# Identity products ahead of the first transpositions, keys before queries, and the second segment's rows normalised on GpSimd

## The reference

```python
xn = layernorm(x)                         # over 256, no scale or shift
q, k, v = split(xn @ Wqkv.T)              # 16 heads of 16; q scaled by 16 ** -0.5
# in each segment of 512 tokens every 8th token is a key: 64 keys for 512 queries
scores = q4 @ k4.T                        # within the segment
c = max(scores over each block of 64 queries, for each key)
w = exp(scores - c);  den = sum(w over keys) + 1e-10
att = (w @ v4 / den) @ Wout.T
ffn = relu(xn @ W1 + b1) @ W2 + b2        # 256 -> 1024 -> 256
out = x + att + ffn
```

## Time and profile before

| | us |
|---|---|
| median of three executions | 1058.35 |
| lowest, highest | 1057.06, 1059.67 |
| profiled execution, time | 1057.22 |
| profiled execution, span from first to last instruction | 1055.3 |
| busy in the span: TensorE, VectorE, ScalarE, GpSimd | 1040.6, 835.4, 648.7, 622.7 |

### The profile page before, as it was taken

How to read it: one execution, slowest core, us unless ns; L and a number is a source line. 1 busy time by engine, 2 the same in 40 slices (tenths; PEclk the granted TensorE clock), 3 DMA queues, 4 the chain that set the end, 5 groups by cost and what they waited for, 6 DMA issues and landing times.

```text
span 1055.3 us, 19263 instructions
## 1 busy us (share of the span) xinstructions
PE 1040.6 (99%) x5397; PEld 809.7 (77%) x5397; DVE 835.4 (79%) x1464; ACT 648.7 (61%) x1081; POOL 622.7 (59%) x491
## 2 busy tenths in 40 slices
PE   6999999999999999999999999999999999999998
PEld 4677778777787777787777787777877777877777
DVE  8977788778888887878878887788888878887753
ACT  5666666656666566665666656566665666656663
POOL 5456655665655666565656656556656565556564
PEclk9999999999999999999999999999999999999999
DMA  5168787787877787877778777879777788768744
GB/s 194 38 160 228 207 234 212 191 216 202 246 216 195 193 216 224 236 206 208 202 213 225 225 204 184 231 201 251 210 192 205 208 229 234 199 175 218 194 145 148
DMA packets 156359, 214.15 MB, mean 203 GB/s; under 512 B 27568, under 2 KB 96304, under 8 KB 156336
## 3 DMA queue, kind: packets, MB, share of 16 engines
q1 hardware_dynamic: 156192, 213.73, 74.4%
q10 hardware_dynamic: 144, 0.13, 0.0%
HBM read 100.01 MB, written 58.20 MB: 150 GB/s over the span
## 4 chain that ended last, share of the span: by engine, by line
PE 92%; DVE 3%; SPq 1%; DMA 1%; issue 1%; ACT 0%; DVEq 0%
PE h_bank L1109 40%; PE y_bank L1109 39%; PE s_banks L1184 5%; PE misc L1288 3%; PE s_banks L1288 3%; PE misc L1109 2%; DVE xn L882 1%; DVE s_max L899 1%; DMA q_pack<-q_hi 1%; DVE w_exp L905 0%; PE misc L1254 0%; PE misc L1226 0%; DMA k_dram<-k_lo 0%; SPq L417 0%; PE s_banks L1195 0%
## 5 line engine op out<-in xcount | busy, mean ns | idle before, releaser
L541 POOL TENSOR_TENSOR h_lo<-h_full,h_hi 128x512 fp32r<-128x512 f32 x256 | 336.9, 1317 | 371.0 <-ACT h_full L646 368.0
L652 ACT ACTIVATE w_exp<-w_exp 128x512 f32<-128x512 f32 x256 | 161.7, 633 | 244.1 <-DVE w_exp L905 242.2
L644 ACT ACTIVATE h_hi<-h_bank,b_cols 128x512 fp32r<-128x512 f32 x256 | 174.8, 683 | 67.7 <-PE h_bank L1109 62.2
L1109 PE MATMUL h_bank<-xt_hi,w_hi 128*128 128x512 f32 x512 | 206.4, 403 | 0.0
L1109 PE MATMUL h_bank<-xt_lo,w_hi 128*128 128x512 f32 x512 | 200.0, 391 | 0.0
L1109 PE MATMUL h_bank<-xt_hi,w_lo 128*128 128x512 f32 x512 | 199.6, 390 | 0.0
L1109 PE MATMUL y_bank<-h_hi,w_hi 128*128 128x512 f32 x496 | 193.4, 390 | 0.2 <-ACT w_exp L652 0.2
L1109 PE MATMUL y_bank<-h_hi,w_lo 128*128 128x512 f32 x496 | 193.1, 389 | 0.0
L1109 PE MATMUL y_bank<-h_lo,w_hi 128*128 128x512 f32 x496 | 193.1, 389 | 0.0
L899 DVE TENSOR_REDUCE s_max<-s_banks 128x8 f32<-128x512 f32 x252 | 169.5, 672 | 28.8 <-PE s_banks L1184 28.4
L905 DVE TENSOR_TENSOR w_exp<-s_banks,s_max 128x512 f32<-128x512 f32 x252 | 174.3, 692 | 10.9
(11 more groups left out here) (149 smaller groups left out, 1540.3 us busy)
## 6 DMA issues: line engine op xcount, KB each, us to landing
q_pack<-q_hi SPq DMA_DIRECT2D x240, 128.0 KB, 2.6
rden_rows<-rden_dram SPq DMA_DIRECT2D x128, 128.0 KB, 4.5
x_b<-x SPq DMA_DIRECT2D x32, 512.0 KB, 4.5
x_raw<-x SPq DMA_DIRECT2D x31, 512.0 KB, 4.8
yt_dram<-y_mem SPq DMA_DIRECT2D x124, 128.0 KB, 3.5
y_mem<-yt_dram SPq DMA_DIRECT2D x62, 256.0 KB, 4.0
out<-x_b SPq DMA_DIRECT2D x31, 512.0 KB, 3.1
q_pack<-q_lo SPq DMA_DIRECT2D x120, 128.0 KB, 2.5
```

Of the source, the lines that this page charges most:

```text
L541: pool.tensor_tensor(h_part[1][:, i % HBUF], h_full[:, i % HBUF], f32(h_part[0][:, i % HBUF]), ALU.subtract).then_inc(h_lo, 1)
L644: act.activation(h_part[0][:, i % HBUF], h_bank[i % 2][:], ACT.Relu, bias=b1_cols[:, i:i + 1]).then_inc(h_hi, 1)
L652: act.activation(w_exp[:, pair], w_exp[:, pair], ACT.Exp).then_inc(w_ready, 1)
L1109: mm = pe.matmul(ps, stationary[a], moving[b], start=start and c == 0 and n == 0, stop=stop and c == len(pairs) - 1 and n == 2, skip_group ...
```

## The change

In the order of the engines:

- TensorE: `raise_clock(count)` issues products of the f32 identity with itself into `h_bank[0]`, which nothing reads: ten before the keys' rows are transposed and two after. `transpose_k` is moved ahead of both halves of the queries. In `lead_step`, `second_product(0, 1)` and the last group of scores are moved ahead of the transposition of segment 1's rows.
- ScalarE: it drains the first key and value sums (`kv_drained`), between the hi parts of the transposed x and of w1. The keys' hi part and the queries' are moved ahead between the weight halves. In `lead_step` it writes segment 0's values into `v` (`first_values`, two copies), behind the second segment's `pair_keys_hi`.
- VectorE: `drain_kv`, `normalise(1, 1)` and `pair_values(-2, 0)` go. `mask_k` comes ahead of the statistics of segment 1, `keys_projected_lo` ahead of the queries' lo parts, and both of these are now in `first_step`. In `lead_step`, the lo part of w2's second half comes behind those of the transposed rows and the keys. A wait for `xn_ready` at 2 is added ahead of `mean_variance(2, 0)`.
- GpSimd: it no longer waits for `xn` before the lo part of w1's second half. In `lead_step` it normalises the rows of segment 1 (`second_rows_normalised`, four `tensor_scalar`) after two `hidden_lo`, and does all five `hidden_lo` before the memset of `q_pack`'s unused rows.

SyncE's code is unchanged.

```diff
--- before.py
+++ after.py
@@ -608,20 +608,31 @@
                     pool.wait_ge(w1_hi[half], 1)
                     if half == 1:
                         inverse_deviation(1, 1)
-                        pool.wait_ge(xn_ready, 2)
                     pool.tensor_tensor(w1_half(w1s[1], half), w1_half(w1_raw, half), f32(w1_half(w1s[0], half)),
                                        ALU.subtract).then_inc(w1_lo[half], 1)
                 pool.wait_ge(w2_hi[0], 1)
                 pool.tensor_tensor(w2_half(w2s[1], 0), w2_half(w2_raw, 0), f32(w2_half(w2s[0], 0)),
                                    ALU.subtract).then_inc(w2_lo[0], 1)
 
+            def second_rows_normalised():
+
+                pool.wait_ge(rstd_ready, 2)
+                pool.wait_ge(xt_psum, DH)
+                for t in range(T):
+                    op = pool.tensor_scalar(xn[:, t], x_raw[:, 1, t], mean_var[:, t, 0:1], rstd[:, t:t + 1],
+                                            ALU.subtract, ALU.mult)
+                op.then_inc(xn_ready, 1)
+
             def lead_step():
-                for i in range(4):
-                    hidden_lo(0, i)
-                pool.wait_ge(h_lo, 4)
+                hidden_lo(0, 0)
+                hidden_lo(0, 1)
+                second_rows_normalised()
+                hidden_lo(0, 2)
+                hidden_lo(0, 3)
+                hidden_lo(0, 4)
+                pool.wait_ge(h_lo, 5)
                 pool.memset(f32(q_pack[PR:P]).rearrange("p n t -> p (n t)"), 0.0).then_inc(pack_zeroed, 1)
                 pool.wait_ge(pack_zeroed, 2)
-                hidden_lo(0, 4)
                 inverse_deviation(2, 0)
                 hidden_lo(0, EARLY)
                 hidden_lo(0, EARLY + 1)
@@ -686,6 +697,18 @@
                 act.wait_ge(q_psum, (s + 2) * DH + m + 1)
                 act.copy(q_part[0][:, m], query_banks(s)[m][:]).then_inc(q_hi, 1)
 
+            def kv_drained(s):
+                act.wait_ge(kv_psum, s + 4)
+                act.copy(kv[:], key_banks(s)[1][:]).then_inc(kv_ready, 2)
+
+            def first_values():
+
+                act.wait_ge(kv_ready, 2)
+                act.wait_ge(masks_zero, 2)
+                for a in range(2):
+                    act.copy(v[a * KEYS:(a + 1) * KEYS, 0].rearrange("p n (d a) -> p n d a", a=2)[:, :, :, a],
+                             kv[0:KEYS, D:].rearrange("p (n a d) -> p n a d", a=2, d=HD)[:, :, a, :]).then_inc(v_ready, 1)
+
             def pair_keys_hi(s, par):
                 act.wait_ge(k_ready, s + 3)
                 act.copy(k_part[0][:], k_full[:, par]).then_inc(k_hi, 1)
@@ -695,12 +718,13 @@
                 keys_hi(-2)
                 weight_hi(wq_raw, wq[0][:], wq_loaded, 16, wq_hi)
                 transposed_hi(-2, 0)
+                kv_drained(-2)
                 weight_hi(w1_half(w1_raw, 0), w1_half(w1s[0], 0), w1_loaded, 16, w1_hi[0])
+                pair_keys_hi(-2, 0)
+                queries_hi(-2, 0)
                 weight_hi(w1_half(w1_raw, 1), w1_half(w1s[0], 1), w1_loaded, 16, w1_hi[1])
-                queries_hi(-2, 0)
+                queries_hi(-2, 1)
                 weight_hi(w2_half(w2_raw, 0), w2_half(w2s[0], 0), w2_loaded, 16, w2_hi[0])
-                pair_keys_hi(-2, 0)
-                queries_hi(-2, 1)
                 weight_hi(w2_half(w2_raw, 1), w2_half(w2s[0], 1), w2_loaded, 16, w2_hi[1])
 
             def lead_step():
@@ -717,6 +741,7 @@
                 exponential(-1, 5)
                 act.wait_ge(s_psum, PAIRS)
                 pair_keys_hi(-1, 1)
+                first_values()
                 hidden(0, 4)
                 weight_hi(wout_raw, wout[0][:], wout_loaded, 64, wout_hi)
                 exponential(-1, 6)
@@ -735,9 +760,8 @@
                 exponential(0, 1)
                 transposed_hi(0, 0)
                 exponential(0, 2)
-                act.wait_ge(kv_psum, 4)
                 act.wait_ge(v_ready, 4)
-                act.copy(kv[:], key_banks(0)[1][:]).then_inc(kv_ready, 2)
+                kv_drained(0)
                 exponential(0, 3)
                 exponential(0, 4)
                 exponential(0, 5)
@@ -1066,35 +1090,33 @@
                 weight_lo(wkv_raw, wkv[0], wkv[1], wkv_hi, wkv_lo)
                 weight_lo(wq_raw, wq[0], wq[1], wq_hi, wq_lo)
                 transposed_lo(-2, 0)
-                drain_kv(-2)
+                mask_k(-2)
                 statistics(1, 1)
                 statistics_done(1)
                 mean_variance(1, 1)
-                mask_k(-2)
+                keys_projected_lo(-2, 0)
                 queries_lo(-2, 0)
-                keys_projected_lo(-2, 0)
-                normalise(1, 1)
+                queries_lo(-2, 1)
 
             def lead_step():
                 for n in range(PAIRS):
                     if n == 0:
                         dve.wait_ge(w1_lo[0], 1)
                     if n == 2:
-                        queries_lo(-2, 1)
                         dve.wait_ge(w1_lo[1], 1)
                     if n == 4:
                         dve.wait_ge(w2_lo[0], 1)
                     if n == 6:
-                        weight_lo(w2_half(w2_raw, 1), w2_half(w2s[0], 1), w2_half(w2s[1], 1), w2_hi[1], w2_lo[1])
                         transposed_lo(-1, 1)
                         keys_projected_lo(-1, 1)
-                        pair_values(-2, 0)
+                        weight_lo(w2_half(w2_raw, 1), w2_half(w2s[0], 1), w2_half(w2s[1], 1), w2_hi[1], w2_lo[1])
                     shift_scores(-1, n)
                 weight_lo(wout_raw, wout[0], wout[1], wout_hi, wout_lo)
                 for m in range(DH):
                     queries_lo(-1, m)
                 statistics(2, 0)
                 statistics_done(2)
+                dve.wait_ge(xn_ready, 2)
                 mean_variance(2, 0)
                 pair_values(-1, 1)
 
@@ -1341,12 +1363,18 @@
             pe.wait_ge(masks_made, 2)
             pe.transpose(s_bank[1][:, 0:P], k_mask_t[:], identity[:]).then_inc(k_mask_psum, 1)
 
+            def raise_clock(count):
+                for _ in range(count):
+                    pe.matmul(h_bank[0][:, 0:P], identity[:], identity[:], start=True, stop=True)
+
             def first_step():
+                raise_clock(10)
                 transpose_keys(-2)
+                raise_clock(2)
                 transpose_x(-2, 0)
                 keys_values(-2)
+                transpose_k(-2)
                 queries(-2, 0, 0)
-                transpose_k(-2)
                 queries(-2, 0, 1)
 
             def lead_step():
@@ -1357,10 +1385,10 @@
                 row_scores(-1, (4, 5), DH, 2)
                 first_product(0, 3, 0)
                 second_product(0, 0)
+                second_product(0, 1)
+                row_scores(-1, (6, 7), DH, 6)
                 pe.wait_ge(s_shifted, 4)
                 transpose_x(-1, 1)
-                second_product(0, 1)
-                row_scores(-1, (6, 7), DH, 6)
                 first_product(0, 4, 0)
                 second_product(0, 2)
                 for m in range(DH):
```

## The result

The changed kernel takes 1061.8 us (median of 14 runs, 1059.87 to 1064.45), the kernel before 1058.67 (14 runs, 1057.06 to 1061.4). The ratio is 1.0026, with a 95% interval from 1.0016 to 1.0036: some 3 us slower, where the prediction had +0.8 and a range up to 1061.2. The profiled executions say the same: 1060.09 us with a span of 1058.0, against 1057.22 and 1055.3.

A forecast was written before the change was run, and what follows sets the result against it. TensorE bounds the regular steps, so only their start moves, set by VectorE's first `s_max`: a 0.4 us early gain, then lead-step delays, put it at 41.3 instead of 40.50. 1058.35 + 0.8 = 1059.15 us, range 1056.8 to 1061.2.

The forecast's parts named there:

- part 3: Lead step: transposition of segment 1's rows starts 1.85 us later, queries 0.6 late, seventh score tile 0.7 late; `s_max` +0.8 us.
- the four normalisations on GpSimd: Lead step: taken at 2.41 us together, `xn` ready at 27.1, hidden by 1.5 us before the transposition at 28.6.
- rival D: Lead step: slow GpSimd normalisations cost one-for-one beyond 3.95 us for four; at 7, +3.9 us, total 1062.2; chance 0.05.
- The identity products: Front of TensorE: twenty passes, 4.2 to 5.0 us, fill idle gaps; cost taken as 0, at most 0.4 us.
- The key products: Front of TensorE: last two run at the 2.4 GHz level and end at 11.5 instead of 12.63.
- `k_lo` is held by GpSimd's subtraction: VectorE, front: `k_lo` held until GpSimd's `w_lo` ends at 16.0, leaving 0.4 us gain; without the hold 1.3.
- The transposition: TensorE, lead step: starts at 28.6 behind an added second product and scores, 1.85 us later than before.
- The copies of the values: ScalarE, lead step: two copies before hidden unit 4, 0.6 us for both, between 0.3 and 0.9.
- the memset: GpSimd: moves from 28.6 to 34.9, beside `wout_lo`; holds no two-tile subtraction, cost 0, 1.8 us if it did.
- Rival B: Front: the early start's gain goes through to the `s_max` at 40.50; -0.5 us, 1057.9; chance 0.27.
- Rival C: TensorE's clock does not rise before 13.4 (+1.6 us) or falls again (+2.8); together 1060.6; chance 0.15.
- Anything else there: Regular steps: something unforeseen, on either side, slower or faster; remaining chance 0.03.

## Why the prediction was wrong

**The step that failed** is in part 3: the four normalisations on GpSimd. I took 2.41 us, the price of one two-input instruction over the same elements, and wrote that even 3.9 would be hidden, so the sum has no term for them. They took 4.85, so `xn` was ready at 29.72, and TensorE stood still for 0.93 us. That is rival D's mechanism, with its point of decision (3.95) confirmed to the tenth: 4.85 - 3.95 = 0.90. I gave it 0.05 since I asked whether it could cost 3.2 us, not whether it could cost one. Putting the step back (with its wait) left +0.72 us in the front, close to the forecast of +0.8. The nearest row by element count hid that the work is four instructions of another form, and no row priced that form. The Trainium skill gives no price for it either: its best case for GpSimd is 512 elements in 769 ns (GPSIMD Engine Reference, 3.1 Elementwise — side-by-side cycle accounting), and an estimate by that pace is 0.38 us for the 256 here; the measured 1.21 decides.

**The steps that held.** The identity products cost nothing and are through before `xn` (twenty passes in 4.48 us, within 4.2 to 5.0). The key products are at the high level. `k_lo` is held by GpSimd's subtraction, 1.06 us long. The first scores start at 17.20 where 17.05 was forecast, with x landing 0.5 us later. The transposition starts 1.26 us after its forecast, of which 0.93 are the wait; behind it everything is shifted by 1.2 to 1.4 us and otherwise as written: `xt_lo` 31.20 (forecast 29.8), seventh score tile 34.51 (33.2), queries 34.97 (33.7), `s_max` 42.48 (41.3). The copies of the values take 0.64 us on ScalarE (forecast 0.6), and the memset holds nothing. The late transposition is a cost of its own: 1.26 us net when undone, so the forecast's +0.8 was this loss less the front's gain.

**Rival B** failed as a forecast for this kernel, but is what remains without parts of the change: with the transposition early and the normalisations on VectorE, `s_max` starts at 40.10. **Rival C** did not come in the changed kernel's two profiles: the key products ran at the upper level. My argument for it, that TensorE has only transpositions between 7.5 and 9.7, left out the two identity products behind the keys' transposition, which ran from 7.45 to 8.28. The Trainium skill's rule (TensorE: Matmul & The Clock Gate, Part 4: PE-mode transpose), that transpositions don't count as activity, therefore isn't tested here: identity products ran ahead of the transpositions of x in all twelve profiles that have them. In eleven the key products ran at the upper level; in the one left it had fallen, and there TensorE's idle time ahead of the keys' transposition, 1.43 us, was the longest of the twelve. What decides it stays open.

**What no step had** is the regular steps. I had read that the chain stays on TensorE there and that a microsecond of the front is one of the total. The chain of that same trace leaves TensorE between 138 and 162 us, beyond the rows I looked at, and the 0.49 us at step 5 show that the front's loss isn't simply carried through. Anything else there had a chance of 0.03. "A difference between the traces that arises after 60 us" was named as what would be wrong, and it arose, about 1.1 us in the profile. Instructions added ahead of the loop remove it from the profile, which speaks for the place of the code as its cause; by what mechanism wasn't tested.

**The sum.** In the profiled pair the front gives 1.46 us, the later landing of x, which the change didn't cause as far as is known, 0.52, and the steps from 5 on 1.1, less the 0.4 by which the offset had fallen at step 5: 2.68, against 2.7 between the spans. Two things stay open. The added instructions take the 1.1 us away in the profile and not in the medians (1061.46 and 1061.26 against 1061.59), so its worth in the time isn't shown. It may be that it is covered there by late DMAs of `q_pack`, for which TensorE waited 0.3 to 1.5 us in all in single executions, at different steps each time. And the two comparisons of the changed kernel, 1.0026 and 1.0017, only just agree. So 1.3 to 1.5 us of the front are shown, 0.6 to 0.7 of them by the failed step and the rest by the late transposition less the front's early start; what the medians (1.9 and 3.1 us apart) have beyond them is left without a shown cause.

## What to carry to other kernels

Price work that moves to another engine by instruction and form, not by elements, and where no row has the form, ask at which price its cover ends and give that point a chance of its own. A wait between engines that looks superfluous may keep one of them off the other's instructions: before taking it out, look at what the other engine runs at that moment. Moving a transposition behind other work of TensorE isn't free merely because TensorE stays busy; what counts is the chain of drains and subtractions behind it.

## What the runs showed of the hardware

- A `tensor_scalar` with two operations and two scalars per partition, 128x256 f32, took 1.21 us on GpSimd (4.85 and 4.83 us for four) and 0.35 on VectorE.
- Four such instructions on VectorE took 7.37 us beside four two-input subtractions running back to back on GpSimd: one was let through at a time.
- After 5.34 us without work TensorE ran at a granted clock of 0.50, from 28.0 to about 33.6 us.
- The first instruction of VectorE's loop started 0.40 us after its release in the two kernels with the changed VectorE program (0.65 in the first pass), and 0.25 to 0.29 in all others, among them two with the same program and only four or eight more instructions ahead of the loop.
- In the fourteen profiled executions TensorE waited for DMAs of `q_pack` between not at all (two of them) and 1.5 us in all, at different steps.
